# A fused attention and mixture-of-experts kernel: another order of the work behind attention, and three tiles of results kept on the chip

## What is computed

```
x = x + attn(_layernorm(x), ctx, ctx, Wq, bq, Wk, bk, Wv, bv, Wo, bo)   # per token, 16 heads of 8
n = _layernorm(x)                                     # [2048, 128]
probs = softmax(n @ router_w)                         # [2048, 8]
expert_gate, expert_index = top_k(probs, 2)
for each token and each of its 2 experts e:
    v = n @ (wv[e] * sv[e])                           # 128 -> 512
    y = gelu(n @ (w[e] * s[e]))                       # 128 -> 512
    out = (v * y) @ (w1[e] * s1[e])                   # 512 -> 128
x = x + sum over the 2 experts of expert_gate * out
```

## Time and profile before

| | |
|---|---|
| median of 3 runs | 257.63 us (256.04 to 260.35) |
| the profiled execution | 256.52 us |
| span of its trace, first to last instruction | 254.7 us |
| outside the span | 1.8 us |
| TensorE busy | 222.4 us (87% of the span) |
| mean granted TensorE clock | 0.957 of 2.4 GHz |

### The profile page before, as it was taken

One profiled execution on the slowest core, in us unless ns is written; L12 is line 12 of the kernel. 1 busy time (PEld: TensorE's weight loads), 2 busy tenths in 40 slices (PEclk: granted clock), 3 DMA queues, 4 the chain that ended last, 5 costly groups with the idle time before them and its releaser, 6 DMA issues.

```text
span 254.7 us, 6311 instructions
## 1 busy us (share of the span) xinstructions
PE 222.4 (87%) x1825; PEld 213.2 (84%) x1826; DVE 182.1 (71%) x436; ACT 130.9 (51%) x362; POOL 144.6 (57%) x158
## 2 busy tenths in 40 slices
PE   7997999997999788957977969999999999999900
PEld 6995988997989688856977969999999999999900
DVE  2699799899899988997356865656656646566471
ACT  2415646668766864736584523645545545455200
POOL 6956646654598689878673454443453535343330
PEclk9999999999999999995799988999999999999985
DMA  4979999999200000012312011122121212000853
GB/s 119 305 147 414 346 319 390 381 378 380 73 23 13 21 31 23 21 42 61 71 52 55 21 35 52 55 64 64 43 65 51 75 55 59 32 18 6 242 155 99
DMA packets 25518, 30.93 MB, mean 121 GB/s; under 512 B 2652, under 2 KB 16896, under 8 KB 25362
## 3 DMA queue, kind: packets, MB, share of 16 engines
q1 hardware_dynamic: 19852, 24.36, 30.7%
q0 software_dynamic: 2528, 4.77, 5.8%
q10 hardware_dynamic: 3110, 1.47, 2.0%
HBM read 16.26 MB, written 14.79 MB: 122 GB/s over the span
## 4 chain that ended last, share of the span: by engine, by line
PE 64%; DVE 18%; issue 6%; DMA 4%; ACT 4%; POOL 2%; DVEq 1%; another core or an unknown queue 1%; POOLq 0%; ACTq 0%; SPq 0%
PE bank L1078 26%; PE bank L1097 12%; PE bank L949 7%; PE bank L996 6%; DVE qk L1221 4%; PE bank L883 3%; DVE pv L336 3%; DMA expert_out<-yo,xs 3%; PE bank L1004 2%; PE bank L1062 2%; ACT w_sb L704 1%; DMA pv<-expert_out 1%; PE bank L958 1%; PE bank L927 1%; PE bank L1007 1%
## 5 line engine op out<-in xcount | busy, mean ns | idle before, releaser
L622 POOL DMA_INDIRECT expert_out<-yo,xs x39 | 40.5, 1039 | 53.7 <-DMA expert_out<-yo,xs 28.2
L336 POOL TENSOR_TENSOR pv<-probs,ctx_sb 128x1408 f32<-128x1408 f32 x14 | 40.1, 2867 | 21.1 <-DVE probs L1272 21.1
L1078 PE MATMUL bank<-xsT,g_tile 128*128 128x128 f32 x312 | 42.7, 281 | 5.4 <-ACT xsT L806 3.1
L580 POOL DMA_INDIRECT routed<-rows,pos x32 | 36.5, 1141 | 17.5 <-DMA routed<-rows,pos 8.0
L1078 PEld LDWEIGHTS bank<-xsT,g_tile 128*128 128x128 f32 x312 | 38.9, 196 | 6.3 <-issue 4.0
L1097 PE MATMUL bank<-w_sb,hid 128*128 x312 | 42.2, 279 | 0.0
L1078 PE MATMUL bank<-xsT,v_tile 128*128 128x128 f32 x312 | 42.2, 279 | 0.0
L1429 DVE TENSOR_TENSOR hid<-bank,act_sb 128x512 f32<-128x512 f32 x39 | 26.9, 690 | 19.2 <-PE bank L1078 13.1
L1420 DVE TENSOR_TENSOR g_tile<-g_sb,g_scale 128x512 f32 x39 | 26.9, 693 | 17.1 <-issue 12.3
L1097 PEld LDWEIGHTS bank<-w_sb,hid 128*128 128x128 f32 x312 | 38.8, 196 | 0.2 <-issue 0.2
L1078 PEld LDWEIGHTS bank<-xsT,v_tile 128*128 128x128 f32 x312 | 38.9, 196 | 0.0
(11 more groups left out here) (191 smaller groups left out, 313.1 us busy)
## 6 DMA issues: line engine op xcount, KB each, us to landing
routed<-pad_rows SPq DMA_DIRECT2D x4, 2080.0 KB, 20.1
xs<-routed SPq DMA_DIRECT2D x39, 65.0 KB
g_sb<-in_L_ffn_w_dram SPq DMA_DIRECT2D x1, 2048.0 KB, 11.1
g_scale<-in_L_ffn_s_dram SPq DMA_DIRECT2D x1, 2048.0 KB, 15.7
v_sb<-in_L_ffn_wv_dram SPq DMA_DIRECT2D x1, 2048.0 KB, 26.5
pv<-expert_out SPq DMA_DIRECT2D x3, 512.0 KB, 5.3
x_sb<-in_x_dram SPq DMA_DIRECT2D x4, 256.0 KB, 6.2
ctx_sb<-in_ctx_dram SPq DMA_DIRECT2D x4, 256.0 KB, 6.2
```

The costliest lines, as they stand in the source:

```text
L336: return eng.tensor_tensor(pv[:, b, g0:g1, :, :], probs[:, b, :, g0:g1].rearrange("p h g -> p g h").unsqueeze(3).to_broadcast([P, many, H, ...
L580: pool.indirect_dma_start(out=routed[:, :], out_offset=bass.IndirectOffsetOnAxis(ap=pos[:, m % TOP, m // TOP:m // TOP + 1], axis=0), in_=r ...
L622: pool.indirect_dma_start(out=expert_out[:, :], out_offset=bass.IndirectOffsetOnAxis(ap=xs_i[:, t % XB, P:P + 1], axis=0), in_=yo[:, t % X ...
L1078: mm = nc.tensor.matmul(psum[:, n * P:n * P + P], weights[:, c % 2, n * P:n * P + P], xsT[:, c % 2, :], start=True, stop=True)
```

## The change

1. **Order at the seam.** TensorE, ScalarE and VectorE run row tiles 0 to 6 closer together; the second normalisation of group 3 and its routing are spread among them and come later. ScalarE does `z_turned(15)` ahead of `normed(3, ...)`. TensorE gets 9 matmuls without use (`keep_warm(9, bank[5])`) behind `output_sum(14)`.
2. **The late table** is cut into six pieces, one behind each of `gated(7)` to `gated(12)` instead of inside tiles 3 to 5, and works on three levels (token tiles up to 12, 14 and 16) where it had two, so its wide operations have 24 columns a tile for 16. `table_ready` is awaited at tile 17 as before.
3. **Indirect DMAs.** Group 2's 8 scatters now go in pairs with a wait between (before: no wait), with the two parts of `second_rstd(3)` and `left_table(True)` between the pairs. Group 3's scatters and the result sends go so that each waits only for the one two before it.
4. **The ring** `xs`/`yo` has `XB` = 18 slots. The code of VectorE's steps is written out (no loop), that of TensorE and ScalarE loops once.
5. **Kept results.** Only tiles 0 to 35 are sent (`SENT` = 36, `KEPT` = 3). The results of tiles 36 to 38 stay in `yo`. They hold only rows of the last two token tiles. For each, GpSimd builds a 128 x 256 matrix of 0 and 1 behind the sends of tiles 27, 28 and 29 (`owners`: 3 operations), and behind `down(38)` TensorE sums in one PSUM bank the residual of the last two token tiles and the three products of `yo` with its matrix. The rows of `expert_out` that belong to those token tiles are cleared early (`cleared`).
6. **The end.** Reading back is in three levels: token tiles 0 to 11 after 31 sends, 12 and 13 after 35, 14 and 15 after 36. VectorE adds token tiles 0 to 11 behind `gated(33)` to `gated(37)`; token tiles 12 to 15 behind `gated(38)`.

The core of the diff:

```diff
+KEPT = 3
+SENT = TILES - KEPT
+OWNERS = 27
-XB = 12
+XB = 18
...
                     for m in range(first, end):
-                        if n >= MID_G and m and m % 2 == 0:
+                        if n == EARLY_G and m and m % 2 == 0:
                             for half in scattered[n]:
                                 pool.wait_ge(half, 16 * (m // 2))
+                        if n >= MID_G and m >= 2:
+                            pool.wait_ge(scattered[n][m % 2], 16 * (m // 2))
...
+                def owners(n):
+
+                    c = (SENT + n) % XB
+                    pool.wait_ge(xs_loaded[c], 16 * ((SENT + n) // XB + 1))
+                    pool.tensor_copy(kept_dest[:, n:n + 1], xs_i[:, c, P:P + 1]).then_inc(token_step, 1)
...
+                    pool.tensor_scalar(not_before[:, :], token_rows[:, :], kept_dest[:, n:n + 1], 0.0,
+                                       ALU.subtract, ALU.is_le).then_inc(token_step, 1)
...
+                    pool.tensor_tensor(whose[:, n, :], not_before[:, 0:LAST * P], not_before[:, 1:],
+                                       ALU.subtract).then_inc(whose_ready, 1)
...
-                for t in range(TILES):
+                for t in range(SENT):
                     pool.wait_ge(yo_ready, t + 1)
-                    if t % 2:
-                        pool.wait_ge(y_sent[(t - 1) % XB], 16 * ((t - 1) // XB + 1))
+                    if t >= 2:
+                        pool.wait_ge(y_sent[(t - 2) % XB], 16 * ((t - 2) // XB + 1))
...
+                    if 0 <= t - OWNERS < KEPT:
+                        owners(t - OWNERS)
...
-                for end, chunks in ((COVER, range(len(CHUNKS) - 1)), (TILES, range(len(CHUNKS) - 1, len(CHUNKS)))):
+                for level, end in enumerate((*COVER, SENT)):
...
+                nc.tensor.matmul(bank[7][:, 0:LAST * P], ident[:, :], x_sb[:, DONE[-2]:, :].rearrange("p t d -> p (t d)"),
+                                 start=True, stop=False)
+                for n in range(KEPT):
...
+                    for m in range(LAST):
+                        mm = nc.tensor.matmul(bank[7][:, m * P:m * P + P], whose[:, n, m * P:m * P + P], yo[:, (SENT + n) % XB, :],
+                                              start=False, stop=(n == KEPT - 1 and m == LAST - 1))
+                mm.then_inc(kept_psum, 1)
...
+                FINAL = {33: (lambda: add_pairs(0),), 34: (lambda: add_rows(0),), 35: (lambda: add_pairs(1),),
+                         36: (lambda: add_rows(1), lambda: add_pairs(2)), 37: (lambda: add_rows(2),)}
+                ffn_steps(dve, ffn, 4, {6: late_ends, 7: late_tiles, 8: late_passed, 9: late_experts, 10: late_offsets, 11: late_rows}, late=FINAL)
+
+                add_pairs(3)
+                add_rows(3)
+                add_pairs(4)
```

255 lines of the change are left out of this document (155 added, 100 removed).

## The result

The changed kernel took 251.6 us (median of 4 runs, 249.34 to 253.64) against 257.41 us for the kernel before beside it (256.04 to 260.35): a ratio of 0.973, 95% interval 0.965 to 0.980. It is faster, as forecast, but the time is 9.9 us over the 241.7 predicted and outside the range of 236.5 to 249.0. The profiled execution took 252.81 us, with a span of 251.1.

What follows compares the result with a forecast made beforehand. TensorE, busy 222 of 254.7 us, was taken as the bound, leaving its idle and slow time, some 32 us, to win. Terms -2.9 - 7.9 + 3.4 + 0.3 - 7.7 = -14.8 from 256.5 gave 241.7 us, range 236.5 to 249.0.

Steps and rivals of the forecast that it cites:

- D: GpSimd's scatters, result sends and owners' steps: send 30 about 0.3 late, +0.3 us, bounds 0 and +3.
- the new rule alone is worth nothing: GpSimd's waiting only for the transfer two before gains nothing, since no TensorE row waited for a send.
- B: Tiles 0 to 9 at the seam: losses of 1.6 us in place of 9.4, so -7.9 us.
- wrong in the forecast if the clock falls within tiles 0 to 16: Sign to look for in the changed kernel's profile: TensorE's granted clock dropping in those tiles would refute the forecast.
- A: Start of the seam: clock kept by idle-filling matmuls, first gate products at about 118.7, -2.9 us.
- C: Late table in six pieces on VectorE: slows the tiles up to tile 15, +3.4 us.
- slower rival: Owners' operations take 2.33 us each, VectorE stops TensorE among the last tiles: 257 us, chance 0.02.
- E: The end: span ends 4.2 us behind the last `yo` in place of 11.86, -7.7 us.
- The seam stays loose: At the seam ScalarE falls 4 or 5 us behind or TensorE's clock falls: 246 to 249 us, chance 0.18.
- VectorE waits among the last tiles: Late send 30 holds `add_pairs(0)`, stopping VectorE and TensorE for 15.6 us: 257 us, chance 0.02.

Runs made afterwards that it cites:

- e1: Changed kernel with group 3's scatters and the result sends both in pairs with a pause again: 255.3 us, ratio 0.985.
- e15: Changed kernel with group 3's scatters and sends 0 to 15 in pairs, owners' steps earlier, read-back additions later: 245.6 us, ratio 0.954.
- e7: Kernel before the change with only group 2's eight scatters put in pairs: 255.5 us against 255.6.
- a2: The changed kernel, unedited, run again on another chip: 239.96 us, ratio 0.951.
- e6: Changed kernel with group 3's scatters and the first 16 sends in pairs, then two always under way: 247.1 us, ratio 0.984.
- e8: Changed kernel with group 3's scatters in pairs and result sends one at a time: 282.9 us, ratio 1.125.
- e9: Changed kernel with group 3's scatters in pairs and the first 24 sends in bursts of eight: 240.5 us, ratio 0.955.
- e5: Changed kernel with group 3's scatters in pairs and the first 24 sends in bursts of four: 239.0 us, ratio 0.952.
- e3: Changed kernel with only group 3's scatters in pairs with a pause, sends left unbroken: 246.7 us, ratio 0.954.
- e13: Changed kernel with group 3's scatters and sends 0 to 15 in pairs, owners behind sends 21, 24 and 27: 245.9 us, ratio 0.977.
- a3: The changed kernel, unedited, run a third time, on a chip with late reports: 252.3 us, ratio 0.971.
- e11: Changed kernel with group 3's scatters in pairs, sends in bursts of four, and without the nine idle-filling matmuls: 240.6 us, ratio 0.957.

## Why the prediction was wrong, point by point

**The step that failed** is in D: "Here the new rule alone is worth nothing: before, no row of TensorE waits for a send either". The term was put at nothing. I looked for those who wait for a send, and found that the rule can gain nothing; I didn't ask what transfers without a pause do to the others. On some chips they make TensorE's reports late, and at the seam three engines in order stand within 10% of each other (B's own words), so each late report stops all. It cost 11.8 us at tile 20 (191.50 against 179.68) and 12.1 in the span (251.1 against 239.0), both between chips of the two kinds; against `e1` and `e15`, on chips that make reports late, it is 10.3 and 10.4 at tile 20. The prediction's own sign came with it: "wrong in the forecast if the clock falls within tiles 0 to 16", and it fell at tiles 8 and 10. A warning of it stood in the trace of before, right behind six scatters of the third group that went out with no pause between 124 and 132: two waits put down to "remote" at 133 us, and the 3.08 before tile 3, which I put down to ScalarE's order. TensorE's report of work that ended at 129.62 came at 133.01 there, 3.4 us late, and the one that VectorE's 1.20 waited for, of 131.47, at 133.17. How much of the 3.08 this made isn't shown; 1.82 is left in `e7`, on a chip without late reports and with that group in pairs. I took all of it for the order of work.

The total is right on a chip that doesn't do this: 240.0 measured, 241.7 predicted. In part that is luck. The sum starts from 256.5 us, a trace with late reports, and takes off 14.8; where none are late, the ratio of 0.951 makes the gain 12.3 us. No trace of the kernel before itself was taken on such a chip, so which of its 14.8 the forecast would lack there stays open. Against the rows of before, the terms can be read one by one in `a2`; the two spans differ by 15.7 (254.7 and 239.0).

- **A**, forecast -2.9, first products 118.7: 119.41, so -2.2; 119.58 and -2.0 in the first trace. The clock was kept, but `value_sum` ended at 118.1 where I had 117.1: VectorE's values came about 1 us later than in the trace of before, which no term had. The 0.7 is less than what the start of the seam varies by: in the sixteen traces with this seam and the nine matmuls the first products start from 117.96 to 120.22.
- **B**, products of tile 9 near 146: 146.38. From the first products to those of tile 9 it took 26.97 where before took 35.66: 8.7 saved, forecast 7.9. Right.
- Behind the second table load ScalarE's next operation starts 0.02 us later in `a2`, as in the earlier trace rows; behind the first it waits 0.47 for VectorE. No drain shows, and tile 9 came within 0.4 of a walk that has none. By the 1.38 us that the Trainium skill adds for it ("ScalarE: Activation LUTs", section "What ACT_TABLE_LOAD costs") the forecast would have been 244.5; the measurement decides against it here.

```profile
131.66 1.28 ACT L720 ACT_TABLE_LOAD   x1
132.96 0.20 ACT L720 ACTIVATE pause_act<-eps 128x1 f32<-128x1 f32 x1
```

- **C**, forecast +3.4, tile 15 at 166.6 by the sum: 165.63. The six tiles from 9 took 3.33, 3.22, 2.95, 3.43, 3.37 and 2.95, in all 19.25 where 16.8 is full: +2.5. Right in kind, 0.9 too dear. The register read was exposed in full, as reckoned (0.78 idle before `g_tile` behind five of the six pieces).
- **D**, apart from the step above: +0.3 forecast; the wait before tile 36 cost 0.6 (3.39 in place of 2.79). Near, but by two errors that offset each other. Three operations of the owners took 0.20 + 1.17 to 1.68 + 0.61 to 0.74, with their gaps 2.2 to 2.7, where I had 1.6: a `TENSOR_SCALAR` of 257 elements took 1.17 to 1.68, not the half of a us that 2 ns an element gives. The three steps with their sends took 3.3, 3.8 and 3.9 for 2.9 reckoned, so send 30 went out about 2.7 late (216.64, its `yo` ready at 213.69) and not 0.3. But the read of 512 KB behind it took 4.00 and not 5.3. The slower rival's 2.33 each didn't come: none of the small operations took that here. What the Trainium skill says of shared interfaces ("GPSIMD Engine Reference", the table at its head) can bear on the 1.68, which began together with VectorE's `g_tile`, an operation that reads two tiles of SBUF; but others that ran beside a `g_tile` took 1.17 to 1.19 (`a2`, `e6`), so these rows don't decide it. In the first trace:

```profile
218.39 0.21 POOL L673 CAST kept_dest<-xs 128x1 f32<-128x1 int32 x1
218.70 1.19 POOL L677 TENSOR_SCALAR ctx_ig<-token_rows,kept_dest 128x257 f32<-128x257 f32 x1
219.97 0.61 POOL L680 TENSOR_TENSOR ctx_sb<-ctx_ig 128x256 f32<-128x256 f32 x1
...
225.93 1.68 POOL L677 TENSOR_SCALAR ctx_ig<-token_rows,kept_dest 128x257 f32<-128x257 f32 x1
```

- **E**, forecast 4.2 behind the last `yo`: 3.9 in both traces of the changed kernel (251.1 - 247.22, and 239.0 - 235.15). Right.

**The rivals.** "The seam stays loose", 246 to 249, named the right place and the clock's fall, but as three engines too tight, which `a2` disproves, and its upper end was 2.6 us short. "VectorE waits among the last tiles" was priced at 15.6 us with 0.02; its mechanism is real, but the changed kernel keeps clear of it. It appears the moment the sends get slower: 4.8 us (`e6`), 11.6 (`e1`), 35.6 (`e8`). So "the rule alone is worth nothing" was wrong in the other direction as well: the rolling rule is what lets the read-back come in time once the seam is tight.

**Which version.** No run beats the changed kernel clearly on a chip without late reports: 240.0, `e9` 240.5, and `e5` 239.0 on another chip, with ratios that overlap. On chips with them pairs to send 15 with the reads later have the best ratio (0.954, and 0.954 for `e3` on another chip, against 0.971 to 0.973), but on a clean chip that pacing in its two nearest forms (`e13`, `e6`) cost 6 to 8 us. Fours are the compromise: equal to the changed kernel on the one kind (0.952), perhaps better on the other (0.962 and 0.964; beside it on one chip 249.3 against 252.3 us, with intervals that overlap).

## What to carry to other kernels

When a change removes a pause, ask who else uses the quiet, not only who waits for the thing that gets faster: late reports showed up as idle time of engines whose producer had long finished. Compare the wait's end with the producer's own row, and take a wait put down to no engine at all, in the trace of before, as a warning with a price. And before a time is explained by an edit, run the unedited kernel beside it on the same chip; four experiments here would have proved a pacing rule that only one kind of chip needs.

## What the runs showed of the hardware

- Chips differ in this. On three of five numbered chips (6, 15, 0) TensorE's semaphore increments reached ScalarE and VectorE up to 9.7 us late (`a3`) while GpSimd issued indirect transfers at one per 1.3 to 1.7 us without a pause; on two (8, 3) none was over 0.3 late, in ten traces. Single runs of the kernel before took 255.0 to 262.1 us on the first three and 250.1 to 256.9 on the others.
- The updates of TensorE's semaphores were themselves late, and came together: in the first trace those for work finished between 141.1 and 143.9 came at 144.82 to 145.13. What holds them back stays open. Pairs with a pause of 2 us took away the waits put down to "remote" (0 us in two traces, of `e1` and `e15`), bursts of four to six didn't; but even with pairs 30 and 27 increments were 0.3 to 1.5 us late, and small waits stayed longer on such a chip (1.02 us before tile 10 in `e15`, 0.38 in `a2`). Whether it is the descriptors that GpSimd writes or the transfers themselves wasn't tried.
- Nine idle-filling matmuls (18 records, 2.17 us) kept the clock at 1.00 over a gap behind which it was 0.50 without them (`a2` and `e11`, 114 to 116 us).
